# A transformer block with routed experts: the expert stages of a fused kernel run one tile deeper

## The chip, the cores and the metric

One Trainium2 chip, one of its cores. The metric is the time on the device, in microseconds, of one execution of the whole program on that core. The input has 8,192 tokens of 128 numbers each, in float32.

## The reference

The program is one block: a feed-forward layer with routed experts, attention, and the same feed-forward layer again.

```python
x = x + 0.5 * ffn(layernorm(x))      # first expert stage
x = x + attention(layernorm(x))
x = x + 0.5 * ffn(layernorm(x))      # second expert stage

def ffn(x):                          # x: 8192 tokens x 128
    top 2 of 8 experts by x @ router;  gate = sigmoid(score of a chosen expert)
    for each chosen expert e:        # xg = gate * x
        out += (silu(xg @ w_in[e]) * (xg @ w_swiglu[e])) @ w_out[e]     # 128 -> 256 -> 128
    out += (silu(x @ w_in_shared.T) * (x @ w_swiglu_shared.T)) @ w_out_shared.T
```

Each token goes to two experts, so an expert stage handles 16,384 pairs of a token and an expert.

## The kernel before, in words

The kernel is a sequence of blocks, each with its own program for every engine; between two blocks all engines meet at a barrier. Block 1 (lines 316 to 694) normalises, routes, computes the shared part and scatters every (token, expert) row to the array `pairs` in HBM, sorted by expert. `experts(0)` (lines 752 to 918) computes the routed part. The third block (from line 922) adds the results to the tokens, does the attention and routes for the second layer; `experts(1)` is the same code again, and a last block (from line 1448) adds up and stores.

**What one expert tile is.** A tile is 256 rows of `pairs` of one expert, held as two halves of 128 rows. There are NT = 71 tiles in each of the two stages. Semaphore counts and ring slots go on from the first stage to the second (`done = NT * ffn`). For tile i:

- SyncE loads the rows into `XS` (line 836, 130 KB), a ring of XB = 8 slots; a load into a used slot waits until the results that were scattered from it have landed (`y_sent`, line 835). Each row brings its gate and the number of its result row.
- ScalarE multiplies each half by the gate into `XG` (`scale`, line 844).
- TensorE transposes the two halves into a PSUM bank (`turn`, line 894).
- ScalarE copies that to `XSH`, rounded to the type float32r (`high`, line 849), and VectorE makes the rest, `XSL` (line 808). VectorE also copies the expert's weights, high and low part, to `WX` (line 811, 128x1024).
- TensorE computes both products of the tile with three matmuls for each of four pieces, 12 matmuls of 256 columns (`up`, lines 886 to 888).
- ScalarE applies SiLU to the first product (`SG`, line 863), VectorE multiplies with the second (`HT`, line 802).
- TensorE multiplies with `w_out` (`down`, line 904, 4 matmuls in full float32, which the trace shows as 8), ScalarE copies the result to `YO` (`send`, line 855, the same ring as `XS`), and GpSimd scatters its two halves to `results` in HBM, one indirect DMA each (line 820).

**What sets the order.** Each engine runs a loop that is written out by hand; the offsets in it are the depth of the pipeline. In iteration i TensorE does `up(i)`, `turn(i+2)`, `down(i-1)` (lines 910 to 918). ScalarE does SiLU of i, first half of `scale(i+3)`, `high(i+2)`, second half of `scale(i+3)`, `send(i-1)` (lines 860 to 871). VectorE does `HT(i)`, `XSL(i+2)`, `WX(i+2)` (lines 798 to 812). `XG`, `XSH`, `XSL`, `WX`, `SG` and `HT` have two buffers each, and PSUM banks 0/1 (turned rows), 2/3 and 4/5 (the two products) and 6/7 (result) are used in turn. The order of the loops makes most reuse of buffers safe without a wait.

**How a stage ends.** GpSimd waits until every scatter has landed (lines 823 and 824), drains, and then releases the barrier (the trace shows this at line 754, the `with` of the block).

## Time and profile before

| | |
|---|---|
| times of the program | 988.44, 991.25, 995.65 us; median 991.25 us |
| the profiled execution | 990.6 us, of it 988.9 us from its first to its last instruction (the span) |
| mean granted TensorE clock | 0.913 of full speed |
| first expert stage | first load issued at 216.54 us, next block's first load issued at 414.94 us |
| second expert stage | results of its first tile copied at 719.28 us |

The profile is of one execution. A timeline row gives start, length, engine, line, operation and names, and in brackets the time that the engine stood idle before it and who released it. PE is TensorE's matmuls, PEld its weight loads, DVE VectorE, ACT ScalarE, POOL GpSimd, SP SyncE; a q behind an engine's name means its instruction queue (waits, register work, DMA issues), which isn't counted as busy time. The length of a GpSimd scatter is the time in which it writes the transfer's descriptors, not that of the transfer.

### The profile page before, as it was taken

How to read it: one execution, taken by the hardware profiler on the slowest of the kernel's cores; microseconds unless marked ns; L12 is line 12 of the kernel's file. 1: busy time of each engine (PE TensorE's matmuls, PEld its weight loads, DVE VectorE, ACT ScalarE, POOL GpSimd, SP SyncE). 2: the span in 40 equal slices, each digit the busy share in tenths (PEclk: the TensorE clock that was granted, in tenths of full speed). 3: DMA queues.
4: the chain of work that ended last, by engine and by line, in shares of the span. 5: the costliest groups of instructions: out<-in, count | busy, mean ns of one | idle time of the engine just before them, and what ended most of it. 6: DMA issues, size and time to landing. Idle time of an engine off the chain costs nothing. (4 is left out here: it accounts for less than half of the span.)

```text
span 988.9 us, 19495 instructions
## 1 busy us (share of the span) xinstructions
PE 835.5 (84%) x5857; PEld 732.3 (74%) x5857; DVE 644.2 (65%) x2022; ACT 573.3 (58%) x1662; POOL 647.2 (65%) x701
## 2 busy tenths in 40 slices
PE   4787777609999999369999999996599999994997
PEld 3676666509999999326776767775499999993886
DVE  6786654506666666157899998885366666661666
ACT  3324232117777777279988888862277777772332
POOL 4777777745777777470688887677367777774421
PEclk9797777959999999779999999996699999997999
DMA  9611111422333333250112211112423333333653
GB/s 233 189 47 44 44 46 43 85 70 71 104 106 102 109 107 102 74 150 22 49 59 75 79 39 40 36 44 63 88 80 103 109 106 109 101 97 109 170 153 105
DMA packets 112920, 88.01 MB, mean 89 GB/s; under 512 B 13426, under 2 KB 102132, under 8 KB 112820
## 3 DMA queue, kind: packets, MB, share of 16 engines
q1 hardware_dynamic: 94816, 51.08, 20.6%
q0 software_dynamic: 17280, 35.69, 10.8%
q8 instruction: 51, 0.84, 0.4%
q14 instruction: 49, 0.40, 0.1%
q10 hardware_dynamic: 724, 0.01, 0.0%
HBM read 43.68 MB, written 43.04 MB: 88 GB/s over the span
## 5 line engine op out<-in xcount | busy, mean ns | idle before, releaser
L820 POOL DMA_INDIRECT results<-YO,XS x284 | 275.6, 970 | 120.5 <-issue 84.7
L802 DVE TENSOR_TENSOR HT<-bank,SG 128x512 f32<-128x512 f32 x142 | 98.1, 691 | 132.9 <-PE bank L888 132.9
L886 PE MATMUL bank<-XSH,WX 128*128 128x256 f32 x568 | 174.1, 306 | 0.3 <-DVE WX L811 0.3
L992 POOL DMA_INDIRECT pairs<-PAY,POS x128 | 134.8, 1053 | 59.0 <-issue 28.8
L411 POOL DMA_INDIRECT pairs<-PAY,POS x128 | 128.3, 1002 | 57.8 <-issue 30.8
L887 PE MATMUL bank<-XSL,WX 128*128 128x256 f32 x568 | 162.0, 285 | 0.0
L888 PE MATMUL bank<-XSH,WX 128*128 128x256 f32 x568 | 161.9, 285 | 0.0
L904 PE MATMUL bank<-WOE,HT 128*128 x1136 | 150.2, 275 | 0.1
L904 PEld LDWEIGHTS bank<-WOE,HT 128*128 128x128 f32 x1136 | 138.1, 192 | 0.5 <-issue 0.5
L844 ACT ACTIVATE XG<-XS 128x128 f32<-128x128 f32 x284 | 111.0, 392 | 44.1 <-DMA XS<-pairs 44.1
L863 ACT ACTIVATE SG<-bank 128x512 f32<-128x512 f32 x142 | 84.9, 598 | 48.8 <-PE bank L888 48.8
L886 PEld LDWEIGHTS bank<-XSH,WX 128*128 128x128 f32 x568 | 110.2, 194 | 1.1 <-issue 1.1
L887 PEld LDWEIGHTS bank<-XSL,WX 128*128 128x128 f32 x568 | 110.7, 195 | 0.0
L888 PEld LDWEIGHTS bank<-XSH,WX 128*128 128x128 f32 x568 | 110.1, 194 | 0.0
L811 DVE CAST WX<-WE 128x1024 fp32r x142 | 97.4, 686 | 0.1
L1215 ACT ACTIVATE PR<-bank,NM 128x128 f32<-128x128 f32 x256 | 90.6, 378 | 1.0 <-DVE NM L1035 1.0
L894 PE MATMUL bank<-ident,XG 128*128 128x128 f32 x284 | 55.8, 279 | 35.0 <-ACT XG L844 35.0
L456 ACT ACTIVATE SSG<-bank 128x512 f32<-128x512 f32 x32 | 19.1, 595 | 113.7 <-PE bank L636 113.7
L808 DVE TENSOR_TENSOR XSL<-bank,XSH 128x256 fp32r<-128x256 f32 x142 | 58.7, 414 | 35.3 <-ACT XSH L849 35.2
L855 ACT ACTIVATE YO<-bank 128x256 f32<-128x256 f32 x142 | 54.7, 385 | 36.4 <-PE bank L904 36.4
L1363 PEld LDWEIGHTS bank<-V,PT 128*128 128x128 f32 x512 | 63.9, 197 | 6.7 <-issue 6.7
L1339 PE MATMUL bank<-KT,QT 128*128 128x512 f32 x128 | 65.7, 596 | 3.0 <-ACT PR L1215 2.5
(197 smaller groups left out, 1760.9 us busy)
## 6 DMA issues: line engine op xcount, KB each, us to landing
XS<-pairs SPq DMA_DIRECT2D x142, 130.0 KB, 2.3
Y<-results SPq DMA_DIRECT2D x32, 256.0 KB, 3.3
YF<-results SPq DMA_DIRECT2D x32, 256.0 KB, 3.4
results<-YO,XS POOLq DMA_INDIRECT x284
pairs<-PAY,POS POOLq DMA_INDIRECT x256, 2.3
out<-X SPq DMA_DIRECT2D x16, 256.0 KB, 2.5
pairs<-pad_rows SPq DMA_DIRECT2D x16, 130.0 KB
pairs<-pad_rows SPq DMA_DIRECT2D x1, 1040.0 KB, 15.3
```

Of the source, the lines that this page charges most:

```text
L411: pool.indirect_dma_start(pairs, bass.IndirectOffsetOnAxis(ap=POS[:, b % RB, j, c:c + 1], axis=0), PAY[:, b % RB, c, j, :], None).then_inc ...
L802: dve.tensor_tensor(HT[:, i % 2, :], bank[4 + i % 2][:, :], SG[:, i % 2, :], ALU.mult)\
L811: dve.tensor_copy(WX[:, i % 2, :, :].rearrange("p h f -> p (h f)"), WE[:, ds(e * 4 * F, 4 * F)]).then_inc(k["e_weights"], 1)
L820: pool.indirect_dma_start(results, bass.IndirectOffsetOnAxis(ap=XS[:, u, j, AT_DEST:AT_DEST + 1].bitcast(U32), axis=0), YO[:, u, j, :], No ...
L844: act.activation(XG[:, i % 2, j, :], XS[:, slot(i), j, 0:D], ACT.Copy, scale=XS[:, slot(i), j, AT_GATE:AT_GATE + 1]).then_inc(k["xs_scaled ...
L863: act.activation(SG[:, i % 2, :], bank[2 + i % 2][:, :], ACT.Silu).then_inc(k["e_silu"], 1)
L886: pe.matmul(ps, WX[:, i % 2, 1, w], hi, start=True, stop=False)
L887: pe.matmul(ps, WX[:, i % 2, 0, w], lo, start=False, stop=False)
L888: mm = pe.matmul(ps, WX[:, i % 2, 0, w], hi, start=False, stop=True)
L904: mm = pe.matmul(chunk(bank[6 + i % 2], j), HT[:, i % 2, (2 * c + j) * P:(2 * c + j + 1) * P], WOE[:, ds(e * FC * D + c * D, D)], start=(c ...
L992: pool.indirect_dma_start(pairs, bass.IndirectOffsetOnAxis(ap=POS[:, b % AB, j, c:c + 1], axis=0), PAY[:, b % AB, c, j, :], None).then_inc ...
L1215: ins = act.activation(PR[:, b % 2, a, g * P:(g + 1) * P], chunk(bank[4 + a % 2], g), ACT.Exp, bias=NM[:, b % 2, a, g:g + 1], accum_out=SU ...
```

## The change

TensorE's iteration i becomes `up(i)`, `turn(i+3)`, `down(i-2)`; ScalarE's SiLU of i, `scale(i+5)` around `high(i+3)`, `send(i-2)`; VectorE's `HT(i)`, `XSL(i+3)`, `WX(i+3)`. The loops start one iteration earlier and end one later. `XG` gets four buffers, `XSH`, `XSL`, `WX` and `HT` three, `XS` and `YO` twelve. Where the order no longer covers a reuse, a wait is added: `up(i)` on the product of tile i-2 (banks 2 to 5), `turn(i)` on `XSL` of tile i-2 (banks 0 and 1), and SiLU of i on the product of tile i-2 (`SG`, which keeps two buffers).

```diff
@@ -50,7 +50,7 @@
     assert D == P and S == W and FC == 2 and E == 8
     CAP = N + 2 * P
     SLOTS = 8
-    XB = 8
+    XB = 12
     NT = TOPK * T // 2 + E - 1
     NW = -(-NT // SLOTS)
     NTAB = NW * SLOTS
@@ -754,12 +754,12 @@
             with ExitStack() as mem, nc.Block() as block:
                 XS = sb(f"XS{ffn}", [P, XB, 2, ROW], mem=mem)
                 YO = sb(f"YO{ffn}", [P, XB, 2, D], mem=mem)
-                XG = sb(f"XG{ffn}", [P, 2, 2, D], mem=mem)
-                XSH = sb(f"XSH{ffn}", [P, 2, 2 * P], F32R, mem=mem)
-                XSL = sb(f"XSL{ffn}", [P, 2, 2 * P], F32R, mem=mem)
-                WX = sb(f"WX{ffn}", [P, 2, 2, 2 * F], F32R, mem=mem)
+                XG = sb(f"XG{ffn}", [P, 4, 2, D], mem=mem)
+                XSH = sb(f"XSH{ffn}", [P, 3, 2 * P], F32R, mem=mem)
+                XSL = sb(f"XSL{ffn}", [P, 3, 2 * P], F32R, mem=mem)
+                WX = sb(f"WX{ffn}", [P, 3, 2, 2 * F], F32R, mem=mem)
                 SG = sb(f"SG{ffn}", [P, 2, FC * 2 * P], mem=mem)
-                HT = sb(f"HT{ffn}", [P, 2, FC * 2 * P], mem=mem)
+                HT = sb(f"HT{ffn}", [P, 3, FC * 2 * P], mem=mem)
 
                 def slot(i):
                     return (done + i) % XB
@@ -795,20 +795,21 @@
                 def _(dve):
                     no = Numbers(dve, "dve")
                     no.ahead(0)
-                    for i in range(-2, NT):
+                    for i in range(-3, NT):
                         if 0 <= i:
                             dve.wait_ge(k["e_silu"], done + i + 1)
                             dve.wait_ge(k["e_up1"], done + i + 1)
-                            dve.tensor_tensor(HT[:, i % 2, :], bank[4 + i % 2][:, :], SG[:, i % 2, :], ALU.mult)\
+                            dve.tensor_tensor(HT[:, i % 3, :], bank[4 + i % 2][:, :], SG[:, i % 2, :], ALU.mult)\
                                .then_inc(k["e_hid"], 1)
+                        if 0 < i + 4 < NT:
+                            no.ahead(i + 4)
                         if i + 3 < NT:
-                            no.ahead(i + 3)
-                        if i + 2 < NT:
-                            dve.wait_ge(k["xs_high"], done + i + 3)
-                            dve.tensor_tensor(XSL[:, i % 2, :], bank[i % 2][:, 0:2 * P], XSH[:, i % 2, :].bitcast(F32),
+                            n = (i + 3) % 3
+                            dve.wait_ge(k["xs_high"], done + i + 4)
+                            dve.tensor_tensor(XSL[:, n, :], bank[(i + 3) % 2][:, 0:2 * P], XSH[:, n, :].bitcast(F32),
                                               ALU.subtract).then_inc(k["xs_low"], 1)
-                            e = no.expert(i + 2)
-                            dve.tensor_copy(WX[:, i % 2, :, :].rearrange("p h f -> p (h f)"),
+                            e = no.expert(i + 3)
+                            dve.tensor_copy(WX[:, n, :, :].rearrange("p h f -> p (h f)"),
                                             WE[:, ds(e * 4 * F, 4 * F)]).then_inc(k["e_weights"], 1)
 
                 @block.gpsimd
@@ -841,12 +842,12 @@
                     def scale(i, j):
                         if j == 0:
                             act.wait_ge(xs_loaded[slot(i)], 16 * (turns(i) + 1))
-                        act.activation(XG[:, i % 2, j, :], XS[:, slot(i), j, 0:D], ACT.Copy,
+                        act.activation(XG[:, i % 4, j, :], XS[:, slot(i), j, 0:D], ACT.Copy,
                                        scale=XS[:, slot(i), j, AT_GATE:AT_GATE + 1]).then_inc(k["xs_scaled"], 1)
 
                     def high(i):
                         act.wait_ge(k["xs_turned"], done + i + 1)
-                        act.activation(XSH[:, i % 2, :], bank[i % 2][:, 0:2 * P], ACT.Copy).then_inc(k["xs_high"], 1)
+                        act.activation(XSH[:, i % 3, :], bank[i % 2][:, 0:2 * P], ACT.Copy).then_inc(k["xs_high"], 1)
 
                     def send(i):
                         act.wait_ge(k["e_down"], done + i + 1)
@@ -855,20 +856,23 @@
                         act.activation(YO[:, slot(i), :, :].rearrange("p j d -> p (j d)"), bank[6 + i % 2][:, 0:2 * D],
                                        ACT.Copy, scale=0.5).then_inc(k["e_out"], 1)
 
-                    scale(0, 0)
-                    scale(0, 1)
-                    for i in range(-2, NT + 1):
+                    for n in range(2):
+                        for j in range(2):
+                            scale(n, j)
+                    for i in range(-3, NT + 2):
                         if 0 <= i < NT:
                             act.wait_ge(k["e_up0"], done + i + 1)
+                            if i >= 2:
+                                act.wait_ge(k["e_hid"], done + i - 1)
                             act.activation(SG[:, i % 2, :], bank[2 + i % 2][:, :], ACT.Silu).then_inc(k["e_silu"], 1)
+                        if i + 5 < NT:
+                            scale(i + 5, 0)
                         if i + 3 < NT:
-                            scale(i + 3, 0)
-                        if i + 2 < NT:
-                            high(i + 2)
-                        if i + 3 < NT:
-                            scale(i + 3, 1)
-                        if 0 <= i - 1 < NT:
-                            send(i - 1)
+                            high(i + 3)
+                        if i + 5 < NT:
+                            scale(i + 5, 1)
+                        if 0 <= i - 2 < NT:
+                            send(i - 2)
 
                 @block.tensor
                 def _(pe):
@@ -876,22 +880,26 @@
                     no = Numbers(pe, "pe")
 
                     def up(i):
-                        hi, lo = XSH[:, i % 2, :], XSL[:, i % 2, :]
+                        hi, lo = XSH[:, i % 3, :], XSL[:, i % 3, :]
                         pe.wait_ge(k["xs_low"], done + i + 1)
                         pe.wait_ge(k["e_weights"], done + i + 1)
+                        if i >= 2:
+                            pe.wait_ge(k["e_hid"], done + i - 1)
                         for g in range(2):
                             for c in range(FC):
                                 w = slice(g * F + c * P, g * F + (c + 1) * P)
                                 ps = bank[2 + 2 * g + i % 2][:, c * 2 * P:(c + 1) * 2 * P]
-                                pe.matmul(ps, WX[:, i % 2, 1, w], hi, start=True, stop=False)
-                                pe.matmul(ps, WX[:, i % 2, 0, w], lo, start=False, stop=False)
-                                mm = pe.matmul(ps, WX[:, i % 2, 0, w], hi, start=False, stop=True)
+                                pe.matmul(ps, WX[:, i % 3, 1, w], hi, start=True, stop=False)
+                                pe.matmul(ps, WX[:, i % 3, 0, w], lo, start=False, stop=False)
+                                mm = pe.matmul(ps, WX[:, i % 3, 0, w], hi, start=False, stop=True)
                             mm.then_inc(k[f"e_up{g}"], 1)
 
                     def turn(i):
                         pe.wait_ge(k["xs_scaled"], 2 * (done + i) + 2)
+                        if i >= 2:
+                            pe.wait_ge(k["xs_low"], done + i - 1)
                         for j in range(2):
-                            mm = pe.transpose(chunk(bank[i % 2], j), XG[:, i % 2, j, :], ident[:, :])
+                            mm = pe.transpose(chunk(bank[i % 2], j), XG[:, i % 4, j, :], ident[:, :])
                         mm.then_inc(k["xs_turned"], 1)
 
                     def down(i):
@@ -902,20 +910,20 @@
                         for j in range(2):
                             for c in range(FC):
                                 mm = pe.matmul(chunk(bank[6 + i % 2], j),
-                                               HT[:, i % 2, (2 * c + j) * P:(2 * c + j + 1) * P],
+                                               HT[:, i % 3, (2 * c + j) * P:(2 * c + j + 1) * P],
                                                WOE[:, ds(e * FC * D + c * D, D)], start=(c == 0), stop=(c == FC - 1))
                         mm.then_inc(k["e_down"], 1)
 
                     no.ahead(0)
-                    for i in range(-2, NT + 1):
+                    for i in range(-3, NT + 2):
                         if 0 <= i < NT:
                             up(i)
                             if i + 1 < NT:
                                 no.ahead(i + 1)
-                        if i + 2 < NT:
-                            turn(i + 2)
-                        if 0 <= i - 1 < NT:
-                            down(i - 1)
+                        if i + 3 < NT:
+                            turn(i + 3)
+                        if 0 <= i - 2 < NT:
+                            down(i - 2)
 
         experts(0)
```

## Rows read from the trace of the kernel before

**Rows 1.** the page, 40 slices of the span, busy tenths of TensorE
```profile
PE   4787777609999999369999999996599999994997
```

**Rows 2.** busy time in four stretches: stretch, length, busy per engine, granted clock, DMA
```profile
216.00:222.00 6.00, 1.48 (x5) 0.71 (x5) 1.02 (x2) 2.29 (x7) 0.00 (x0) 0.50 0.66 149
222.00:226.00 4.00, 4.00 (x20) 4.00 (x21) 2.04 (x4) 2.00 (x6) 0.00 (x0) 0.53 0.17 44
235.00:400.00 165.00, 165.00 (x1428) 165.00 (x1427) 105.33 (x195) 125.26 (x322) 125.36 (x131) 1.00 0.37 103
726.00:890.00 164.00, 164.00 (x1419) 164.00 (x1419) 104.89 (x195) 124.57 (x321) 124.68 (x130) 1.00 0.37 104
```

**Rows 3.** the page, costliest groups: busy, mean ns, idle before and releaser
```profile
L820 POOL DMA_INDIRECT results<-YO,XS x284 | 275.6, 970 | 120.5 <-issue 84.7
...
L886 PE MATMUL bank<-XSH,WX 128*128 128x256 f32 x568 | 174.1, 306 | 0.3 <-DVE WX L811 0.3
...
L887 PE MATMUL bank<-XSL,WX 128*128 128x256 f32 x568 | 162.0, 285 | 0.0
```

**Rows 4.** the timeline, one tile in the steady part, TensorE weight loads
```profile
301.66 0.19 PEld L886 LDWEIGHTS bank<-XSH,WX 128*128 128x128 f32 x1
...
303.10 0.24 PEld L894 LDWEIGHTS bank<-ident,XG 128*128 128x128 f32 x2
...
303.31 0.97 PEld L904 LDWEIGHTS bank<-WOE,HT 128*128 128x128 f32 x8
...
304.20 0.19 PEld L886 LDWEIGHTS bank<-XSH,WX 128*128 128x128 f32 x1
```

**Rows 5.** the timeline, result copy and next free scatter, early and late
```profile
230.66 0.38 ACT L855 ACTIVATE YO<-bank 128x256 f32<-128x256 f32 x1 [0.22 <-PE bank L904]
...
231.66 0.97 POOL L820 DMA_INDIRECT results<-YO,XS  x1 [0.30 <-issue]
...
386.00 0.39 ACT L855 ACTIVATE YO<-bank 128x256 f32<-128x256 f32 x1 [0.22 <-PE bank L904]
...
387.01 0.97 POOL L820 DMA_INDIRECT results<-YO,XS  x1 [0.31 <-issue]
```

**Rows 6.** the timeline, start of the first expert stage
```profile
216.54 4.79 SPq L836 DMA_DIRECT2D XS<-pairs  x8
...
219.88 0.40 ACT L844 ACTIVATE XG<-XS 128x128 f32<-128x128 f32 x1 [0.34 <-DMA XS<-pairs]
220.31 0.38 ACT L849 ACTIVATE XSH<-bank 128x256 fp32r<-128x256 f32 x1
220.59 0.68 ACT L844 ACTIVATE XG<-XS 128x128 f32<-128x128 f32 x2
...
221.07 0.68 DVE L811 CAST WX<-WE 128x1024 fp32r x1
...
221.90 0.55 PE L886 MATMUL bank<-XSH,WX 128*128 128x256 f32 x1 [0.17 <-DVE WX L811]
...
228.78 0.97 POOL L820 DMA_INDIRECT results<-YO,XS  x1 [17.50 <-ACT YO L855]
```

**Rows 7.** the timeline, end of the first expert stage
```profile
404.60 0.38 ACT L855 ACTIVATE YO<-bank 128x256 f32<-128x256 f32 x1 [0.82 <-PE bank L904]
...
408.64 0.96 POOL L820 DMA_INDIRECT results<-YO,XS  x1 [0.30 <-DMA results<-YO,XS]
414.94 16.54 SPq L960 DMA_DIRECT2D Y<-results  x12
```

**Rows 8.** instructions of lines 881, 886, 854, 754: ns min/median/max, first and last start
```profile
L881 PEldq EVENT_SEMAPHORE  x142: 51/51/51, 221.8 to 890.5; - x142
...
L886 PE MATMUL bank<-XSH,WX x568: 280/283/562, 221.9 to 893.1; 128*128 128x256 f32 x190
...
L854 ACTq EVENT_SEMAPHORE  x134: 17/17/17, 247.6 to 894.6; - x134
...
L754 POOLq DRAIN  x2: 3467/3472/3477, 411.2 to 902.4; - x2
```


## The prediction

> **What bounds the kernel now.** I read the page's slices first, then the stretches of the two expert stages, then the groups, and then single tiles in the timeline. In the slices TensorE has two long plateaus of nines [rows 1]: these are the expert stages, the only code that the change touches. Inside them TensorE is busy for 165.00 of 165.00 us and for 164.00 of 164.00 us, its weight loads as well, at a granted clock of 1.00, its upper level of 2.4 GHz [rows 2]. VectorE (105.33 of 165 us) and ScalarE (125.26) have room. So no matmul in the steady part waits for a buffer, which is what a deeper pipeline could cure.
>
> One tile is, in weight loads, 1.44 us of `up`, 0.21 of `turn` and 0.89 of `down`, and the next tile's `up` begins 2.54 us after this one's [rows 4]. Over the stage this holds exactly: the result copies of tiles 1 and 62 are 155.34 us apart, 2.547 us a tile [rows 5].
>
> A second engine stands right beside it. GpSimd writes two scatters per tile, 0.97 us each with 0.30 between them [rows 3, 5], so a pair takes 2.54 us: practically TensorE's period. The scatter of a tile begins 0.62 us after the end of its result copy at tile 1 and again 0.62 us after it at tile 62 [rows 5]. GpSimd has no room, but doesn't fall behind while results come every 2.547 us. At the end they come faster (tiles with no `turn`, then with no `up`) and GpSimd can't follow: the last result copy ends at 404.98 us, the last scatter's descriptors at 409.60, and the next block begins at 414.94 after landing, waits and a drain of 3.47 us on GpSimd [rows 7, 8]. So a stage's length is: time to its first result, then 142 scatters at GpSimd's pace, then the landing and the drain. TensorE's pace and GpSimd's are equal in the middle; at the end GpSimd alone decides.
>
> **The change part by part.**
>
> *First results later, by `down` one tile further behind.* Before the first `down` TensorE now also does `up(2)` and one more `turn`. `up(2)` begins two tiles after `up(0)`, some 5 us on, when the clock should have risen (0.53 from 222 to 226 us, 1.00 later [rows 2]), so I price both as in the steady part: 1.44 + 0.21 = 1.65 us [rows 4]. Bounds: nothing, if they filled a gap; but TensorE runs through from 221.90 us [rows 2, 6]. And up to 3.2 us, if both fell into the lower level, at which the stretch from 222 to 226 us ran (clock 0.53, half speed) [rows 2]. I take 1.65, from the nearest row.
>
> *The start itself, by gating ahead.* ScalarE now gates two tiles before its loop and then the first half of the third before `high(0)`. The order was second tile's first half (219.88 us, held up by its load), `high(0)` at 220.31. It becomes: that half, its second half, the third tile's first half, `high(0)`. Starts of such copies lie some 0.30 us apart (two in 0.68) [rows 6], so `high(0)` starts at 219.88 + 3 x 0.30 = 220.78, 0.47 later. `XSL(0)` and `WX(0)` follow it, and `up(0)` was released by `WX(0)` [rows 6], so `up(0)` starts 0.47 later too, at 222.37. The third `turn`, which now stands before `up(0)`, has its rows by about 221.45 and fits in. Bounds: 0 if `high` weren't what `up(0)` waits for, 1.2 if the third tile's load is late (loads are issued every 0.6 us or so, eight in 4.79 us [rows 6]; the third came in time for its copy before, and is wanted 0.5 us sooner now). I take 0.47.
>
> *The end.* The first scatter moves by 1.65 + 0.47 = 2.12 us, and all results after it, since TensorE's period is unchanged. GpSimd has the same 142 scatters at the same pace behind it, so the last scatter, the drain and the barrier move by 2.12 us as well. The last result copy comes only 0.47 us later; it had ended 4.6 us ahead of the last descriptors [rows 7], and now ends 6.3 us ahead. Two stages: 4.24 us.
>
> *The added waits.* `up` and `turn` of tiles 2 to 70 each get one more: 2 x 69 x 2 = 276 on TensorE's queue. A wait of this kind takes 51 ns there [rows 8]. Behind it the whole matmul stream is queued, so it costs nothing only while the queue runs ahead of the array. It does: the last wait of line 881 ran at 890.5 us, and the last matmul of line 886, the tenth of its tile, started at 893.1; nine steps of 0.12 us back, that tile's first one was at 892.0, 1.5 us after its wait [rows 4, 8]. The conditions are old by then: the product of tile i-2 was there before `up(i-1)`, `XSL(i-2)` long before. I take 0; bounds 0 and 276 x 0.051 = 14.1 us. SiLU's new wait is 17 ns on ScalarE [rows 8], where 40 of 165 us are free [rows 2]: 0.
>
> *More buffers, rings of twelve.* They take no instruction. SyncE issues four more loads before it has to wait for scatters; they are wanted many microseconds later. Loads weren't late in the steady part (TensorE never waited), so nothing is won; the DMA engines are 0.37 busy there [rows 2], so nothing is lost. GpSimd's waits at the end go through twelve counters in place of eight, mostly before the last landing: below 0.2 us, taken as 0. The same operations fill all the engines otherwise.
>
> *Sum*, against the profiled execution: 990.6 + 4.24 = 994.8 us. The three times before are 988.44 to 995.65 with a median of 991.25, so the profiled one lies 0.65 below the median; I forecast 995.0.
>
> **One rule of the skill against the trace.** In the steady part the weight loads of `up` lie 0.120 us apart (1.44 us for 12) [rows 4]. The Trainium skill (TensorE: Matmul & The Clock Gate, section Back-to-back issue gap) gives about N/2.4 + 2.5 ns between single matmuls at full clock, 109 ns for 256 columns, and says itself that streams of weight load and matmul keep another pace. Were the rest waiting that a deeper pipeline removes, 1,704 matmuls x 11 ns would come to an estimated 19 us, by that page alone. The row speaks against it: the spacing is the same for all eleven steps of a tile, and a late buffer would show at the first.
>
> **The rivals.**
>
> *The added waits are paid (slower).* Place: TensorE's queue, between `down` and `up`, and before `turn`. If the lead of 1.5 us isn't free time but is needed to feed the array, every instruction more on the queue is a gap in front of the array. Price: 14.1 us on top of the forecast, 1009. It decides from the point where the queue's work for a tile reaches 2.547 us. Against it: the waits and register steps that the queue has now leave no trace in the weight loads' spacing. For it: TensorE has nothing else that could hide them.
>
> *There is a hidden wait at each tile's first matmul (faster).* Line 886's matmuls take 306 ns in the mean, line 887's of the same size 285 [rows 3]; the surplus sits in the first of a tile. If that is a semaphore that comes late (`XSL` or `WX`), the extra tile of lead removes 568 x 21 ns = 11.9 us: 994.8 - 11.9 = 982.9. Against it: the groups show 0.3 us of idle in all before it [rows 3], and weight loads are busy without a gap too [rows 2]. A wider form: if all twelve steps of `up` could go at the 0.111 us of `down`'s eight (0.89 / 8 [rows 4]), the gain would be 12 x 0.009 x 142 = 15.3 us, and the time 979.5; I give that 0.01 of the chance. It is what the page's rule above would amount to.
>
> *The later first result is made up (no change).* If GpSimd can write faster than a pair in 2.54 us once results pile up, only the start's 0.47 us per stage remains: 991.5. Against it: in the last tiles results did pile up, and its spacing stayed at 1.27.
>
> *GpSimd becomes slower by what lies beside it (slower).* Its margin is about 2 ns per tile. A disturbance of 20 ns in each pair would cost 71 x 2 x 0.02 = 2.8 us: 997.6. The place of the scatters beside VectorE's copy of the weights in a tile's period doesn't change, since all moved by whole tiles.
>
> **How the numbers follow.** A measurement of this kernel can tell about 1% from no change. Chances: the forecast 0.60 (993 to 998 with the spread of the runs), made up 0.14, GpSimd slower 0.07, the waits paid 0.11 (in part or whole), the hidden wait 0.08. The first three lie within 1% (981.3 to 1001.2 us by the median), 0.81 together. Faster by over 1% is only a hidden wait that goes nearly whole, 0.07; slower by over 1% is the waits paid, with a little for what I don't see, 0.12. The range holds 8 in 10: from 989 (made up, in a quick run) to 1001 (a third to a half of the waits paid).
>
> **What would show it right or wrong.** Right: the first scatter of each stage about 2.1 us later, measured from the stage's first load; TensorE still busy throughout with 2.55 us a tile; result to scatter 0.62 us in the middle, and some 4.0 us in place of 2.4 at the last tile (404.98 to 407.37 us now [rows 7]); line 886's mean still 306 ns. A period other than 2.547 us proves the forecast wrong, by 1.4 us in the total for every 10 ns; longer means the waits, shorter the hidden wait. If the last scatter moves by only 0.5 us, GpSimd had room.

## The result and the profile after

The changed kernel takes 995.49 us (median of 20 runs, 993.09 to 997.20), the kernel before 991.87 us in the runs beside them (20 runs, 986.94 to 1001.61). The ratio is 1.0039, 95% interval 1.0020 to 1.0058: 0.2 to 0.6% slower, inside the 1% that I had called no change. The profiled execution has a span of 992.8 us against 988.9.

The page of the changed kernel, its slices and costliest groups. The plateaus of nines are where they were, line 892 (886 before) still has a mean of 306 ns and line 893 one of 285, as in [rows 3]; in the mean no `up` matmul got faster.

```profile
PE   4787777519999999269999999987599999992997
...
L821 POOL DMA_INDIRECT results<-YO,XS x284 | 275.4, 970 | 124.5 <-issue 82.9
...
L892 PE MATMUL bank<-XSH,WX 128*128 128x256 f32 x568 | 173.7, 306 | 0.0
...
L893 PE MATMUL bank<-XSL,WX 128*128 128x256 f32 x568 | 161.7, 285 | 0.0
```

The same two stretches as in [rows 2]: TensorE busy for all of both at a granted clock of 1.00.

```profile
235.00:400.00 165.00, 165.00 (x1429) 165.00 (x1428) 103.61 (x192) 123.39 (x316) 125.68 (x130) 1.00 0.36 101
726.00:890.00 164.00, 164.00 (x1420) 164.00 (x1419) 104.15 (x193) 123.18 (x316) 124.99 (x129) 1.00 0.36 101
```

One tile in the steady part, TensorE's weight loads, as in [rows 4]: from one `up` to the next 2.54 us.

```profile
302.53 0.19 PEld L892 LDWEIGHTS bank<-XSH,WX 128*128 128x128 f32 x1
...
303.96 0.25 PEld L902 LDWEIGHTS bank<-ident,XG 128*128 128x128 f32 x2
...
304.18 0.97 PEld L912 LDWEIGHTS bank<-WOE,HT 128*128 128x128 f32 x8
...
305.07 0.19 PEld L892 LDWEIGHTS bank<-XSH,WX 128*128 128x128 f32 x1
```

The start of the first expert stage, which answers to [rows 6]. ScalarE now does five gatings in a row before `high(0)` (line 850), twelve loads go out, and the first scatter comes at 229.69 us.

```profile
215.00 7.70 SPq L837 DMA_DIRECT2D XS<-pairs  x12
217.21 2.06 ACT L845 ACTIVATE XG<-XS 128x128 f32<-128x128 f32 x5 [26.78 <-DMA XS<-pairs]
...
219.17 0.36 ACT L850 ACTIVATE XSH<-bank 128x256 fp32r<-128x256 f32 x1
...
220.74 0.55 PE L892 MATMUL bank<-XSH,WX 128*128 128x256 f32 x1
...
229.03 0.39 ACT L856 ACTIVATE YO<-bank 128x256 f32<-128x256 f32 x1 [0.22 <-PE bank L912]
...
229.69 0.96 POOL L821 DMA_INDIRECT results<-YO,XS  x1 [19.92 <-ACT YO L856]
```

The end of that stage, as in [rows 7]: GpSimd's last scatter now begins 5.8 us after the end of the last result copy (before: 3.7 us), and the next block's load comes 6.94 us after that scatter (before: 6.30).

```profile
403.27 0.38 ACT L856 ACTIVATE YO<-bank 128x256 f32<-128x256 f32 x1 [0.55 <-PE bank L912]
...
409.45 0.96 POOL L821 DMA_INDIRECT results<-YO,XS  x1 [0.30 <-DMA results<-YO,XS]
416.39 15.73 SPq L968 DMA_DIRECT2D Y<-results  x11
```

And the queues' own instructions, as in [rows 8]: there are two events of 51 ns per tile on TensorE's queue where there was one, and the drain on GpSimd is 4.13 us in place of 3.47.

```profile
L887 PEldq EVENT_SEMAPHORE  x138: 51/51/51, 224.5 to 889.2; - x138
...
L900 PEldq EVENT_SEMAPHORE  x138: 51/51/51, 220.0 to 883.6; - x138
...
L754 POOLq DRAIN  x2: 4121/4126/4131, 412.0 to 904.3; - x2
```

The marks of the two stages in both kernels, in microseconds from each stage's first load:

| | before, first / second stage | changed, first / second |
|---|---|---|
| `high(0)` | 3.77 / 3.74 | 4.17 / 4.06 |
| first `up` (weight load) | 5.33 / 5.30 | 5.71 / 5.60 |
| first scatter | 12.23 / 12.48 | 14.69 / 13.94 |
| last scatter | 192.10 / 192.28 | 194.45 / 193.61 |
| next block's first load | 198.39 / 198.65 | 201.39 / 200.62 |

So the two stages together are 4.97 us longer. The rest of the program is 1.1 us shorter in this pair of profiles, though its code is the same: that is how well two profiles agree.

### The profile page after: what moved, and what is told of

Same layout as the page of the kernel before. It is cut to its first block and busy times, and to the rows that moved or that the text cites. A ratio compares the mean times of both kernels' runs of the same rounds, so it can differ in the third digit from the quotient of the medians.

```text
span 992.8 us, 19767 instructions
## 1 busy us (share of the span) xinstructions
PE 834.5 (84%) x5857; PEld 731.0 (74%) x5857; DVE 645.9 (65%) x2022; ACT 573.5 (58%) x1662; POOL 643.6 (65%) x701
## 5 line engine op out<-in xcount | busy, mean ns | idle before, releaser
L1371 PE MATMUL bank<-V,PT 128*128 128x128 f32 x512 | 67.7, 281 | 0.0
```

The costliest lines, as they stand in the source:

```text
L1371: mm = pe.matmul(chunk(bank[2], a), PT[:, a % 2, g * P:(g + 1) * P], V[:, b % 2, g, :], start=False, stop=(a == BT - 1 and g == G - 1))
```

## The experiments

Twelve kernels ran. Four of them (`e1_down_later`, `e2_rows_ahead`, `e3_ring12`, `e4_ring16`) ran on a chip on which the kernel before took 1071.87 us (one run) and, in the traces of these four, every engine stood still now and then inside the expert stages; below it is called the disturbed chip. On it I read only what lies outside those stretches (starts, drains) and no times of the whole program. All others ran where the kernel before took 988.5 to 991 us. `e8_changed_again` was the changed kernel as the measure beside the others.

> The changed kernel itself, as the measure for the others on this chip. On a chip where the kernel before takes about 991 us: 995; drain 4.13 us, first scatter 14 to 14.7 us after the first load. On a chip where the transfers or queues stall now and then, the deeper loops could be worth more or less than that: no number from theory, the comparison with the kernel before tells.

It took 994.80 us against 990.79 for the kernel before (10 and 31 runs), ratio 1.0033 (1.0003 to 1.0062), first scatters at 14.94 and 14.18 us, drain 4.13 us: the result repeats.

### What the later start costs, and why it was two experiments

```diff
-                        if 0 <= i - 1 < NT:
-                            down(i - 1)
+                        if 0 <= i - 2 < NT:
+                            down(i - 2)
```

(`send` likewise, with HT in three buffers, loops that end one iteration later, and the waits on `e_hid` that the order then needs; ring of eight.)

> The kernel before with only `down` and `send` moved one tile further behind (HT three buffers, ring of 8 kept, the two waits that this needs). My theory: the first scatter comes one `up` and one `turn` later than before, 1.65 us at the upper clock (between 1.2 and 2.1 us, by where the clock rises), the last scatter as much, and the drain on GpSimd stays 3.47 us; so a stage, from its first load to the next block's first load, grows from 198.5 us to about 200.1. Rival (GpSimd makes it up): first scatter later, last scatter where it was, stage 198.5. Rival (all of the loss comes from gating ahead): nothing moves.

First scatter at 13.55 and 13.53 us, drain 3.47 us. The ring experiments below, on the same chip and with `down` one tile behind, had it at 11.51 to 11.70: about 1.9 us, inside the range. The last scatter couldn't be read there. So the same kernel again:

> `down` and `send` one tile further behind and nothing else, again, for a chip on which TensorE runs through. First scatter 1.65 us (1.2 to 2.1) later than in the kernel before, at 13.9 to 14.3 us after the first load, last scatter as much later, at 193.8 us or a little less, drain 3.47 us, stage about 200.1 us. Two stages: 3.3 us more, a ratio of 1.0033. Rival (GpSimd makes up for it): 192.2 and 198.5 us.

First scatters at 13.52 and 13.61 us, 1.29 and 1.13 us later than before: at and below the lower edge (the clock went up early in both, 2.9 and 3.1 us after the first `up`, against 3.9 and 4.6 before). But the kernel took 1027.63 us (4 runs) against 988.50, ratio 1.0381 (1.0335 to 1.0428), not 1.0033. The loss was over ten times the expected one, and the waits of the stretch from 235 to 400 us say where:

```profile
ACT XG L844 <- DMA XS<-pairs: 59.2, 52, 2.7
```

Gating waits for loads: 59.2 us in 52 waits, 2.7 us the longest. The timeline shows the loop (the load, SPq, stands last):

```profile
302.23 0.37 ACT L855 ACTIVATE YO<-bank 128x256 f32<-128x256 f32 x1
...
302.88 1.06 POOL L820 DMA_INDIRECT results<-YO,XS  x1 [0.58 <-ACT YO L855]
...
304.24 0.97 POOL L820 DMA_INDIRECT results<-YO,XS  x1 [0.30 <-issue]
...
309.13 0.40 ACT L844 ACTIVATE XG<-XS 128x128 f32<-128x128 f32 x1 [0.92 <-DMA XS<-pairs]
...
310.00 0.37 ACT L855 ACTIVATE YO<-bank 128x256 f32<-128x256 f32 x1
...
306.90 0.37 SPq L836 DMA_DIRECT2D XS<-pairs  x1
```

The result copy of a tile begins at 302.23 us; its second scatter begins at 304.24; that slot's load can be issued at 306.90, once the scatter has landed; the gating of the tile eight later begins at 309.13, and the result copy three tiles after the first, which ScalarE does behind it, at 310.00. That is 7.77 us for three tiles, 2.59 us a tile, above TensorE's 2.547. Over the stages it was 2.85 and 2.78 us a tile from first to last scatter, more than this one loop gives; the waits come unevenly, and some scatters took over 1.2 us in place of 0.97. What counts is the number of iterations between a tile's send and the gating of the tile that takes its slot: ring minus tiles gated ahead minus tiles sent behind. Before it is 8 - 3 - 1 = 4, here 8 - 3 - 2 = 3, in the changed kernel 12 - 5 - 2 = 5. By this one loop four would do for periods down to an estimated 1.94 us, three only down to 2.59. That is a bound for scatters of usual length and no more: one stage with four iterations, in the run with moved buffers below, did wait for loads. With five (the changed kernel, twice, fourfold waits, eight semaphores) no gating waited for a load after the first tiles.

### Gating and turning ahead alone

The changed kernel with `down(i - 1)` and `send(i - 1)` as before, and without the waits on `e_hid`.

> The changed kernel with `down` and `send` back at one tile behind: rows gated five and turned three tiles ahead, ring of 12. My theory: the first scatter comes 0.3 to 0.5 us later than before (later `high` of the first tile), and the drain is 4.13 us as in the changed kernel, 0.65 more than before: a stage of about 199.5 us. If the longer drain comes from `down` lying one tile further behind, it is 3.47 us here and the stage 198.9.

`high(0)` at 4.28 and 4.05 us against 3.65 to 3.80 in the three others of that chip, first scatters at 12.73 and 12.54 us, 1.0 us after those of the ring experiments; the drain is 4.13 us. So the longer drain isn't due to `down`. The shift was larger than my 0.3 to 0.5. `up(0)` started 0.4 to 0.5 us later, as expected; TensorE then took 0.6 us longer to the first result. In that part it does the same work in both orders, but its clock went to the upper level 3.93 and 4.04 us after the first `up`, and 2.55 to 2.78 us after it in the ring experiments. Whether gating ahead delays the clock, or it fell so here, these runs don't show; the clock's price is worked out under the prediction's second point.

### The rings and the drain

```diff
-    XB = 8
+    XB = 12
```

> The kernel before with rings of twelve slots and nothing else. Theory: the drain on GpSimd grows with the number of slots (each has its own semaphore for the scatters), so it is 4.13 us here against 3.47, a stage is 0.65 us longer and first and last scatter stay where they were after the first load (12.2 and 192.1 us). Rival: the drain depends on the depth of the loops and stays 3.47 us. TensorE's period: 2.547 us if the new pattern of 2.537 to 2.554 us comes from the third buffers, changed if it comes from where the buffers lie in SBUF.

> The kernel before with rings of sixteen slots. If the drain grows evenly with the slots, it is 3.47 + 8 x 0.163 = 4.78 us; if it is a step between eight and twelve, 4.13 us; if the slots have nothing to do with it, 3.47 us. Nothing else should move.

Twelve slots: 4.12 and 4.13 us of drain, with the loops of before. Sixteen slots, GpSimd's queue at the end of the block (line 754):

```profile
L754 POOLq DRAIN  x2: 4774/4779/4784, 446.7 to 976.3; - x2
```

8, 12 and 16 slots give 3.47, 4.13 and 4.78 us: 0.163 us per slot. Is it the loads' slots, or those of the results with their semaphores? The changed kernel with loads in a ring of twelve and results in one of eight:

```diff
-        y_sent = sems("y_sent", XB)
+        y_sent = sems("y_sent", YB)
...
-                YO = sb(f"YO{ffn}", [P, XB, 2, D], mem=mem)
+                YO = sb(f"YO{ffn}", [P, YB, 2, D], mem=mem)
```

> The changed kernel, its loads still in a ring of twelve, but results and the semaphores of the scatters in a ring of eight. If the drain on GpSimd grows with the number of scatter semaphores (or result slots), it is 3.47 us here, and a stage 0.65 us shorter than in the changed kernel; if it grows with the loads' ring, it stays 4.13 us. The first scatter stays at 14 to 15 us after the first load, the period at 2.545 us.

```profile
L755 POOLq DRAIN  x2: 3467/3472/3477, 413.6 to 904.9; - x2
```

3.47 us again, with first scatters at 14.62 and 13.66 us and a period of 2.545 us. It is the results' side: the slots of `YO` or their semaphores; these two I didn't part. From last scatter to the next block it takes 6.31 and 6.37 us here, as before the change. (A single run: 993.47 us.) The second stage, 199.72 us, is shorter by the 0.65 us and a little more; the first isn't (202.14 us), because its last scatter came 181.2 us after its first, and not 179.7 to 179.9. The next experiment has such a stage too.

### The added waits

```diff
                         if i >= 2:
-                            pe.wait_ge(k["e_hid"], done + i - 1)
+                            for _ in range(4):
+                                pe.wait_ge(k["e_hid"], done + i - 1)
```

(The same for the wait on `xs_low` in `turn`.)

> The changed kernel with each of the two waits that it added on TensorE issued four times in place of once: 3 x 276 = 828 more waits of 51 ns. Theory (the queue runs 1.5 us ahead of the array, so waits that are long satisfied cost nothing): period of a tile 2.545 us as in the changed kernel, no longer stage. Rival (waits are paid): 828 x 0.051 = 42 us more in all, 0.30 us a tile. Between the two: the lead is used up by 0.31 us of work on the queue per tile, and the period grows by less than 0.3 us.

```profile
L888 PEldq EVENT_SEMAPHORE  x414: 51/51/51, 223.5 to 890.7; - x138
...
L902 PEldq EVENT_SEMAPHORE  x276: 51/51/51, 219.1 to 885.0; - x138
```

Two conditions share one event, so the fourfold waits became 414 more events and not 828, worth 21.1 us if they were paid. They weren't: the program took 995.28 us (10 runs) against the changed kernel's 994.80 on the same chip, the period stayed 2.545 us, and TensorE is as busy as before:

```profile
235.00:400.00 165.00, 165.00 (x1428) 165.00 (x1427) 104.16 (x192) 122.85 (x314) 125.66 (x130) 1.00 0.36 100
```

Waits on conditions that are long fulfilled are free here, up to 0.15 us more per tile at the least. This also rules out the rival that they decide the result.

The first stage of this run shows something else. Within its first eight tiles several scatters took 1.3 to 1.4 us, and from then on the scatters lay 1.89 us behind the result copies in place of 0.62. The last two rows are tile 62:

```profile
229.95 1.32 POOL L821 DMA_INDIRECT results<-YO,XS  x1 [0.30 <-issue]
...
232.84 1.28 POOL L821 DMA_INDIRECT results<-YO,XS  x1 [0.30 <-issue]
...
235.71 1.38 POOL L821 DMA_INDIRECT results<-YO,XS  x1 [0.30 <-issue]
...
385.81 0.39 ACT L856 ACTIVATE YO<-bank 128x256 f32<-128x256 f32 x1 [0.22 <-PE bank L914]
...
388.08 0.98 POOL L821 DMA_INDIRECT results<-YO,XS  x1 [0.30 <-issue]
```

The 1.27 us lost at the start were all there 54 tiles later, and the last scatter came 195.55 us after the first load. So GpSimd makes up nothing while results come every 2.545 us. Of the fourteen stages of the kernel before, the changed kernel (two runs), this one, the one with eight semaphores and the two with a changed start, three lost 0.9 to 1.5 us by such spells of longer scatters (this one, and the first stages with eight semaphores and with the changed start alone). What lengthens the scatters is open.

### What the 2.545 us are made of

The tiles of the changed kernel take 2.554, 2.537, 2.547 and 2.542 us in turn, where every tile before took 2.547 or 2.546.

```diff
                 XS = sb(f"XS{ffn}", [P, XB, 2, ROW], mem=mem)
+                sb(f"pad0{ffn}", [P, 4, 2, ROW], mem=mem)
```

(Five more such gaps, so that all buffers start where the changed kernel's do.)

> The kernel before, with unused memory between its buffers so that they start where the changed kernel's do; depth, rings and counts of buffers unchanged. If TensorE's pattern of 2.537 to 2.554 us a tile in the changed kernel comes from where the buffers lie, it shows here too; if it comes from the third buffers, only their first two addresses are used here and the period stays 2.547 us or takes two of the values. Worth 0.1 us a stage at most either way: the question is what a period is made of.

Second stage of this kernel, ScalarE's copies to `XSH` of successive tiles:

```profile
800.96 0.38 ACT L855 ACTIVATE XSH<-bank 128x256 fp32r<-128x256 f32 x1
...
803.50 0.38 ACT L855 ACTIVATE XSH<-bank 128x256 fp32r<-128x256 f32 x1
...
806.04 0.38 ACT L855 ACTIVATE XSH<-bank 128x256 fp32r<-128x256 f32 x1
...
808.60 0.38 ACT L855 ACTIVATE XSH<-bank 128x256 fp32r<-128x256 f32 x1
...
811.13 0.38 ACT L855 ACTIVATE XSH<-bank 128x256 fp32r<-128x256 f32 x1
```

The steps in exact starts are 2.536, 2.548, 2.542 and 2.554 us: the changed kernel's pattern, and the third buffers aren't its cause. In three of the four tiles the steps between the `up` matmuls' weight loads, some 0.120 us, differ from those of the kernel before by up to 0.005 us; so they depend in their last nanoseconds on where buffers lie. Why the pattern repeats after four tiles, when `XG`, `XSH`, `XSL`, `WX` and `HT` have two buffers each here, isn't shown.

The first stage of this run took 206.5 us, with 2.62 us a tile, so its single time of 994.38 us says nothing of the pattern; the second stage took 198.51 us, like before. The slow stage says something of the ring. Its loops are those of before, with four iterations between send and gating, and yet (stretch from 225 to 410 us):

```profile
ACT XG L850 <- DMA XS<-pairs: 38.9, 44, 2.1
```

Its scatters took 1.03 us in the mean in place of 0.97, 16 of them over 1.2 us. What began it is open, as above; but four iterations were not enough for it.

### How small the ring may be

> The changed kernel with rings of ten in place of twelve. From the send of tile i to the gating of tile i+10 lie: 0.6 us to its first scatter, 1.27 to the second, 2.25 to its landing, some 0.4 to the issue of the load and 2.3 to 3.4 to its landing, then 1.2 us of ScalarE's iteration: 8.0 to 9.1 us for three iterations. Theory: the ring becomes the bound, 2.7 to 3.0 us a tile in place of 2.545, the program 22 to 65 us longer than the changed kernel. Rival (two slots are spare): 2.545 us and no change but a drain of 3.80 us.

1031.01 us in a single run, inside the 22 to 65 us more that I had expected, and 2.86 and 2.77 us a tile. The waits of the stretch from 235 to 400 us:

```profile
ACT XG L845 <- DMA XS<-pairs: 64.6, 48, 3.4
```

10 - 5 - 2 = 3 iterations between send and gating, and the same picture as with `down` later on a ring of eight: two kernels of different depth and ring, with the same difference, lose 39 and 36 us. The drain is on the line too:

```profile
L754 POOLq DRAIN  x2: 3794/3799/3804, 434.0 to 941.4; - x2
```

### Can the start and the end be had back?

The kernel before, with VectorE copying the first tile's weights before it waits for rows, and ScalarE doing `high(0)` before it gates the second tile:

```diff
+                    weights(0)
                     for i in range(-2, NT):
...
+                        if i == -2:
+                            high(0)
                         if i + 3 < NT:
                             scale(i + 3, 0)
```

> The kernel before with the start of a stage shortened: VectorE copies the first tile's weights before it waits for rows, and ScalarE does `high(0)` before it gates the second tile. Theory: the stage's length is the time to the first result plus 142 scatters plus the tail, so what comes off the start comes off the stage: `up(0)` starts at about 4.5 us after the first load in place of 5.3, first and last scatter 0.7 us earlier, two stages 1.4 us in all (0.1%, below what the times of the whole program can tell). Rival: GpSimd or a load holds the first result anyway, nothing moves.

```profile
214.30 4.80 SPq L842 DMA_DIRECT2D XS<-pairs  x8
...
218.11 0.38 ACT L855 ACTIVATE XSH<-bank 128x256 fp32r<-128x256 f32 x1 [0.78 <-PE bank L902]
...
226.92 0.97 POOL L826 DMA_INDIRECT results<-YO,XS  x1 [17.86 <-ACT YO L861]
```

`high(0)` begins 3.81 us after the first load, as before: it waits for TensorE to turn the tile, not for ScalarE's gating. `up(0)` came 0.23 and 0.29 us earlier, in place of 0.7 to 0.8, and the first scatter 0.4 and 0.3 us later: 12.62 and 12.79 us. TensorE's clock rose later: in both stages 22 steps of `up` matmuls ran at the lower level, against 15 and 18 in the kernel before. 990.69 us, ratio 0.9996 (0.9960 to 1.0031). The expectation failed. The next kernel has the same start and an earlier clock: `up(0)` 0.31 and 0.33 us earlier, and first scatters at 11.96 and 11.69 us, 0.27 and 0.80 us earlier than before. So the edit is worth some 0.3 us a stage, and the rest of either result is the clock. The first stage of `e6_prologue` also ended later than before by more than its start (last scatter at 193.37 us), with scatters of over 1.0 us in its last third.

The same start, and the waits for the scatters' landing moved from GpSimd to SyncE in the next block:

> The same, and the waits for the scatters' landing go from GpSimd at the end of a stage to SyncE at the start of the next block, ahead of its first load of results. Theory: GpSimd's drain of 3.47 us then starts right behind the last scatter's descriptors, 1.6 us earlier, and a stage's end moves by that: 1.6 us more per stage, 4.6 us in all for both edits against the kernel before, a ratio of 0.995. Rival: the drain itself waits for the landing and grows by what it starts earlier; then nothing comes on top of the first edit.

```profile
406.65 0.97 POOL L826 DMA_INDIRECT results<-YO,XS  x1 [0.30 <-issue]
...
411.61 20.65 SPq L968 DMA_DIRECT2D Y<-results  x14
...
L754 POOLq DRAIN  x2: 8008/8044/8081, 403.0 to 891.4; - x2
```

The next block's load comes 4.96 us after the last scatter, in both stages, where it took 6.30 and 6.37 us before: 1.3 to 1.4 us each, of 1.6 expected. The drain reads 8.0 us because its queue entry now begins while scatters are still being written (from 403.0 us on); measured from the last scatter's start it ends earlier. The two stages take 393.26 us together against 397.04 in the kernel before. About 1.1 us of these 3.8 are earlier first scatters, some 0.6 of it by the start and the rest by the clock. The program: 988.26 us (10 runs, 983.22 to 993.95) against 990.79, ratio 0.9979 (0.9941 to 1.0016), so not told from the kernel before; the profiled execution was one of its quick ones, 984.81 us. Against the changed kernel's 994.80 it is 6.5 us less.

## Why the prediction was right, point by point

**TensorE runs through; no gain from depth.** Held: busy 165.00 of 165.00 us after as before, line 886/892 at 306 ns both times. The hidden wait is out: nothing became faster that a buffer could have held up. The prediction had also set the trace's 0.120 us per matmul beside the 0.109 us that the Trainium skill (TensorE: Matmul & The Clock Gate, section Back-to-back issue gap) gives for a single one of 256 columns; those 11 ns aren't waiting that more depth removes either. One reading of mine was too neat: the eleven steps of a tile aren't the same, the first is 0.112 us and the next three are 0.117 to 0.120.

**The period stays 2.547 us.** Nearly: it is 2.545. I had said that any other value would speak for waits or for a hidden wait. It was neither; the padding run shows the same steps with the old loops. Worth 0.26 us over 142 tiles.

**`down` one tile later, 1.65 us.** Held, once the clock is taken out. The part from the first `up` to the first result copy took 8.32 and 7.69 us in the changed kernel's profile against 6.25 and 6.53: 2.07 us in one stage and 1.16 in the other. The difference is where in it TensorE's clock goes from its lower level to its upper one, which shows in the weight loads, here in the kernel before:

```profile
225.45 0.33 PEld L886 LDWEIGHTS bank<-XSH,WX 128*128 128x128 f32 x1
225.67 0.26 PEld L887 LDWEIGHTS bank<-XSL,WX 128*128 128x128 f32 x1
225.86 0.19 PEld L888 LDWEIGHTS bank<-XSH,WX 128*128 128x128 f32 x1
```

The steps are 0.213 us up to there and 0.120 behind it. Sorted by that moment, the stages of all traces but two fall on two lines:

| | clock at its upper level, us after the first `up` | first `up` to first result copy |
|---|---|---|
| `down` one tile behind | 2.64 (ring of 16), 3.92 and 4.57 (before), 5.85 (changed start) | 5.66, 6.25, 6.53, 7.12 |
| rows ahead, `down` two behind | 2.63 (ring of 10), 3.45 and 4.89 (changed), 5.59 (ring of 10) | 7.30, 7.69, 8.32, 8.63 |

Every microsecond that the clock rises later costs 0.45 us, and at the same moment the lines lie 1.64 us apart (14 stages on the first, within 0.05 us of it, and 10 on the second, within 0.01). That is one `up` and one `turn` at the upper level, as priced. With `down` later and nothing else (`e1_down_later`, `e11_down_again`) it is 1.8 us: there TensorE also stands for 0.16 us before `up(2)`, until VectorE has copied that tile's weights. The moment itself was 4.7 and 2.4 us in the two stages of one and the same run (eight semaphores), so in a single pair of profiles 1 us either way is chance.

**Gating ahead, 0.47 us.** Measured 0.38 and 0.30 at `up(0)`. The mechanism was right, but `high(0)` had waited for TensorE's `turn` and not only for its place in the queue, as the run with the changed start showed. That two more gatings fill part of this wait would account for the smaller shift; no run parts it.

**GpSimd carries the shift to the end.** Held: first scatter +2.46 and +1.46 us (forecast 2.12), last scatter +2.35 and +1.33. The 0.1 us between is about what TensorE's shorter period gives. GpSimd made up nothing; in the middle of the stages a scatter follows its result copy by 0.62 to 0.65 us, as forecast, and at the last tile the distance grew to 4.5 and 4.4 us (forecast 4.0). That the first stage's 2.46 and the second's 1.46 lie around my 2.12 is the clock again. The rival in which GpSimd gets slower didn't act in this pair, but it is real: see the fourfold waits.

**The added waits are free.** Held, with 414 events more to spare. Of my 276 waits only 138 became additional events, as two conditions fit into one.

**The rings cost nothing.** This step failed, twice. "GpSimd's waits at the end go through twelve counters in place of eight ... below 0.2 us" was right for the waits, but the drain behind them grew by 0.65 us a stage, 1.3 us in all, a third of the slowdown. And "nothing is won" was wrong as a reading of the ring: with ten slots in place of twelve the deeper loops cost 36 us (1031 us, a single run); eight slots, which leave one iteration, weren't tried. Loads weren't late before because the distance was four iterations; the change without its rings would have made it fewer, and with them it is five.

**The sum.** 4.24 us forecast. In the traces: 3.68 at the last scatter, 1.3 in the tail, 4.97 for both stages, less 1.1 us elsewhere, 3.9 in the span. The medians differ by 3.6 us, and in the repeat by 4.0. The forecast of 995.0 against 995.49 owes part of its closeness to luck: a drain of 1.3 us was left out, 1.1 us came back in blocks whose code didn't change, and in the two stages the clock's chances, +0.4 and -0.5 us, nearly cancelled. The 995.0 itself lies between 994.8, the sum from the profiled run, and 995.5, the same sum from the median of 991.25.

## What to carry to other kernels

Before deepening a pipeline, look whether the engine that sets the pace ever waits. If it is busy for all of the steady part, as here, more depth only moves the first result back, and where another engine with the same pace follows behind, that move reaches the end whole. Count a ring not by its slots but by the iterations that are left between freeing a slot and needing it (slots minus tiles taken ahead minus tiles released behind), and compare them with the time of the whole loop through the DMAs; of eight stages here with only one iteration to spare, one fell behind and lost 8 us, and with two to spare none did. Read the tail of a stage too: what happens after the last work item can depend on a constant that looks like mere memory. And before reading a start-up time from one pair of profiles, note when the clock rose in each.

## What the runs showed of the hardware that was not expected

- The drain of GpSimd's queue at the end of a block with 71 tiles, 142 scatters, takes 3.47, 3.80, 4.13 and 4.78 us with 8, 10, 12 and 16 result slots and semaphores, 0.163 us for each; with twelve load slots and eight result slots it takes 3.47. The line does not carry over to the other blocks: it would give 2.82 us at four, and the block before the expert stage, with four semaphores for 128 scatters, drains in 2.68 us, the attention block, with three, in 2.00.
- Where the buffers lie in SBUF changes the 12 `up` steps of a tile between 1.434 and 1.449 us (1.444 before) and the whole tile between 2.536 and 2.555, in a pattern that repeats after four tiles, also where all of TensorE's operands have two buffers.
- Scatters of 0.97 us take 1.0 to 1.5 us now and then. Half of the normal ones lie beside VectorE's copy of the weights too; in the slow first stage of the run with moved buffers those over 1.2 us had 0.54 us of it beside them in the mean, the normal ones 0.20. That this copy is the cause isn't shown.
- On another chip the kernel before took 1071.87 us in place of 991; its relatives' traces there show all engines halting at times in the expert stages. What causes it is open. With one run each, the old loops took 1064.5 us with rings of twelve and 1067.4 with rings of sixteen, `down` later 1074.3, rows ahead 1072.7: nothing here brings it near 991.
- From the first matmul of a stage it took 2.4 to 5.9 us (10 to 22 steps of `up`) until the granted clock was at its upper level, and in stages with the same code 2.4 and 4.7. Each microsecond costs 0.45 us. This alone moves a stage by 1 us or more and hid the gain of a start that was 0.3 us quicker. What decides the moment is open.
